# Eighteen matmuls that nobody reads, placed between a first attention layer and the routing of a soft mixture of experts

## The reference

```python
h = jnp.concatenate([tok_embed(x), txt], axis=1)               # 32 x 96 x 192
h = h + attn0(layernorm(h))                                    # 12 heads of 16
# soft mixture of experts, 64 slots
xn = rms_norm(layernorm(h), norm_weight); tok = l2_normalize(xn)
logits = einsum('sd,btd->bst', l2_normalize(slots) * scale, tok)
dispatch_w = softmax(logits, axis=-1); combine_w = softmax(logits, axis=-2)
y = einsum('btd,bst->bsd', xn, dispatch_w)
y = gelu(einsum('sio,bsi->bso', fc1_weight, y) + fc1_bias)      # 64 expert matrices 192 x 768
y = einsum('sio,bsi->bso', fc2_weight, y) + fc2_bias
h = h + einsum('bsd,bst->btd', y, combine_w)
# then a causal attention with rotary positions and a routed mixture of 8 experts
```

## Time and profile before

| | us |
|---|---|
| median of 3 runs | 1104.42 (1103.48 to 1104.73) |
| profiled execution | 1107.96 |
| its span | 1105.9 |
| TensorE busy | 854.4 |
| VectorE busy | 603.4 |
| ScalarE busy | 432.1 |
| GpSimd busy | 398.7 |
| mean granted clock of TensorE, 1 being 2.4 GHz | 0.842 |

### The profile page before, as it was taken

One profiled execution on the slowest core, in us unless ns is written; L12 is line 12 of the kernel. 1 busy time (PEld: TensorE's weight loads), 2 busy tenths in 40 slices (PEclk: granted clock), 3 DMA queues, 4 the chain that ended last, 5 costly groups with the idle time before them and its releaser, 6 DMA issues. The chain is left out here.

```text
span 1105.9 us, 23004 instructions
## 1 busy us (share of the span) xinstructions
PE 854.4 (77%) x7560; PEld 704.6 (64%) x7561; DVE 603.4 (55%) x1401; ACT 432.1 (39%) x1022; POOL 398.7 (36%) x390
## 2 busy tenths in 40 slices
PE   3599999999977980444445599889157999999994
PEld 2477887878667960222223467667156999999994
DVE  1657777777753610111111668887794656555552
ACT  5245555545554320000001047764442444444442
POOL 1345444454301300000000026674275565555552
PEclk9689999999955575666668789999557999999998
DMA  9490000000000039989994190000432333332331
GB/s 286 133 409 1 1 0 0 0 0 0 1 1 2 2 113 364 368 361 355 338 336 114 32 399 2 0 0 1 132 79 61 51 50 51 52 50 49 53 53 19
DMA packets 38126, 119.42 MB, mean 108 GB/s; under 512 B 7538, under 2 KB 28564, under 8 KB 33716
## 3 DMA queue, kind: packets, MB, share of 16 engines
q1 hardware_dynamic: 25108, 104.40, 25.6%
q0 software_dynamic: 10848, 12.67, 7.1%
q10 hardware_dynamic: 2112, 1.57, 1.0%
HBM read 105.87 MB, written 11.14 MB: 106 GB/s over the span
## 5 line engine op out<-in xcount | busy, mean ns | idle before, releaser
L1029 PE MATMUL psum<-flat,m_yT 64*32 64x384 f32 x624 | 48.0, 671 | 104.3 <-issue 103.0
L1646 POOL DMA_INDIRECT out_h<-x_ys,idx x55 | 87.3, 1587 | 98.9 <-ACT x_ys L1671 79.3
L1770 PE MATMUL psum<-w_pairs,x_h_hi 128*128 x330 | 101.7, 370 | 1.1 <-DVE x_h_lo L1698 1.1
L1029 PEld LDWEIGHTS psum<-flat,m_yT 64*32 64x32 f32 x624 | 17.7, 143 | 130.0 <-issue 130.0
L986 DVE COPY f_hid<-psum 128x384 f32<-128x384 f32 x16 | 8.9, 558 | 148.7 <-PE psum L1029 148.7
L1222 POOL MEMSET b_ones<- 96x96 f32 x1 | 0.2, 178 | 242.8 <-POOLq L122 242.8
L1772 PE MATMUL psum<-w_pairs,x_h_lo 128*128 x330 | 82.8, 251 | 0.0
L1698 DVE TENSOR_TENSOR x_h_lo<-psum,x_h_hi 128x384 fp32r<-128x384 f32 x110 | 56.3, 553 | 38.8 <-ACT x_h_hi L1667 36.8
L464 POOL TENSOR_TENSOR a_kb<-a_qk,a_hmask 96x576 f32<-96x576 f32 x64 | 72.2, 1147 | 6.2 <-ACT a_qk L497 6.2
L622 PE MATMUL psum<-a_kb,a_qk 96*96 96x384 f32 (+1 forms) x256 | 67.7, 407 | 0.0
L550 DVE TENSOR_REDUCE a_mx<-psum 96x12 f32<-96x1152 f32 x32 | 43.3, 1354 | 41.8 <-PE psum L622 41.8
(11 more groups left out here) (274 smaller groups left out, 2460.2 us busy)
## 6 DMA issues: line engine op xcount, KB each, us to landing
flat<-in_slot_w SPq DMA_DIRECT2D x27, 2304.0 KB, 21.7
ring_last<-in_slot_w SPq DMA_DIRECT2D x5, 2304.0 KB, 27.9
flat<-in_moe_w SPq DMA_DIRECT2D x1, 10752.0 KB, 29.7
flat<-in_x_patches SPq DMA_DIRECT2D x4, 1536.0 KB, 14.6
out_h<-flat SPq DMA_DIRECT2D x1, 2304.0 KB, 12.2
xtab<-flat SPq DMA_DIRECT2D x4, 576.0 KB, 4.0
m_y<-in_fc_b SPq DMA_DIRECT2D x1, 1536.0 KB, 18.4
m_y<-f_y2g ACTq DMA_DIRECT2D x16, 96.0 KB
```

Source lines behind the costliest of these rows:

```text
L1029: mm = pe.matmul(b_h[n][r][B * c:B * (c + 1), :], g.yT[rows, k, SC * gr + c, :], w1[c // 2][rows, c % 2, k, n * N2:(n + 1) * N2], start=(k ...
L1646: pool.indirect_dma_start(out=A["out"][:, :], out_offset=bass.IndirectOffsetOnAxis(ap=g.idx[:, i:i + 1], axis=0), in_=ys[:, i % 2, :], in_ ...
L1770: pe.matmul(b_y[u % 2], h_hi[:, k, :], g.w_pairs[:, :, k, bass.ds(e, 1), :].rearrange("p two a d -> p two (a d)"), start=(k == 0), stop=False)
```

## The change

A function `keep_clock` is added. It issues matmuls of the 128x128 identity with 384 columns of the ring's first buffer, into PSUM bank 3, and nobody reads what they write. It is called twice, both times on PE: with 14 at the end of `attention0`'s block, behind a wait until DVE has read the last scores, and with 4 at the start of the PE stream of `dispatch`. Nothing else changes.

```diff
+N_CLOCK = 384
...
             steps(pe, B, [(project, 1), (turn_first, 3), (score, 2), (transpose_x, 0), (attend, 3), (output, 4)])
+            pe.wait_ge(s_sub, B)
+            keep_clock(pe, g, 14)
...
+def keep_clock(pe, g, n):
+    pe.wait_ge(g.s_ring[0], 16)
+    for _ in range(n):
+        pe.matmul(g.ps[:, 3, 0:N_CLOCK], g.ident[:, :], g.ring[0][:, 0:N_CLOCK], start=True, stop=True)
...
+            keep_clock(pe, g, 4)
             few_steps(NP, [(transpose_x, 0), (products, 1)])
             few_steps(NQ, [(transpose_logits, 0), (transpose_weights, 2), (gather, 3)])
```

## The result

Over 20 executions of each kernel the median went from 1106.76 us to 1110.13; the ratio is 1.003, with a 95% interval from 1.0016 to 1.0044. So the change makes the kernel slower by 3.3 us, between 1.8 and 4.9. The forecast was +7.8 us, with a range for the time that holds the result. Part of that is luck: the forecast time of 1112.2 us counted from 1104.42, the median of three runs, while the comparison's own median before is 1106.76, which is 2.3 us more. So the time came close, and the change itself did not: +3.3 against +7.8. The profiled execution took 1111.2 us with a span of 1109.1, against a span of 1105.9 before.

The account below looks back on a forecast made before the run. The prediction took PE, at half clock through the uncovered `dispatch`, as the bound. A start 8.8 us later less 1.0 given back makes +7.8 on 1104.42, so 1112.2 us, range 1103.6 to 1114.0.

Parts of the forecast that it names:

- The bound and the stage: `dispatch`: all 82 us to `slot_ffn`'s first matmul run at 1.2 GHz, uncovered, so its end shifts the rest equally.
- The rise: From the last output matmuls at 309.62, the clock rises between 313.3 and 315.4 us, taken as 314.4.
- The fourteen: Added matmuls at `attention0`'s end: two done at 1.30 us, twelve at 0.65, ending at 322.2 us, in a 4.70 us gap.
- The barrier and the four: Start of `dispatch`: barrier opens at about 322.7, four matmuls take 2.6 us, first transpose at 325.3, 8.8 us later.
- What the high clock gives back: First part of `dispatch`: each full-clock pair gives back 0.51 us; the clock falls at some 330, four pairs give 1.0.
- My own sign: In the changed kernel's profile, the granted clock reads 0.50 again by 331 us, until `slot_ffn`'s first matmuls at 406.
- falls midway: Rival: in `dispatch`'s first part the clock falls after ten pairs or so; +4 us, 1108.4, chance 0.04.
- the likeliest case: Clock falls early in `dispatch`'s first part; +7.8 us, 1112.2, own range 1109.5 to 1113.5, chance 0.66.
- ACT's 1.35 us a pair: First part of `dispatch` at full clock: ACT's copy and two squares set the pace, 1.35 us a pair against 1.86.
- My first rival: Clock holds to the end of `dispatch`'s first part, all sixteen pairs at ACT's pace; +0.6 us, 1105.0, chance 0.18.
- The second part: Later part of `dispatch`, where PE first has only a few transposes a chunk: priced at no change, 0.
- The case on the other side: Rival: the clock holds through both parts of `dispatch`; -17.4 us in all, 1087, chance 0.08.

Follow-up runs that it names:

- the best run: Against the kernel before: two unread matmuls ahead of the barrier, four behind, one or more late in `dispatch`'s second-part steps, ACT's first part written out; 1086.95 us, ratio 0.9827.
- the run with transposes: Changed kernel with each unread 384-column matmul replaced by six unread 128x128 transposes; ratio 1.006 to the kernel before.
- the run with three chunks filled: Kernel before plus four matmuls behind the barrier, ACT's first part written out, two more in each of chunks 0 to 2 of `dispatch`'s second part; ratio 0.9985.

## Where the prediction was right and where wrong

- **The bound and the stage.** Right. `dispatch` ran at half clock, lost at the attention's end or in the gap behind it, and what moved in `dispatch` moved the end: +4.17 at `slot_ffn`'s start in the profile and +3.3 in the comparison, -19.0 and -19.4 in the best run.
- **The rise.** Right. I took 3.7 to 5.8 us from the start of the last output matmuls and chose 4.8; it rose after 3.7. In the runs with fourteen matmuls or with transposes it rose after 3.0 to 3.9, so my lower bound was too high.
- **The fourteen.** Right. Forecast 10.4 us, measured 10.0. They overran PE's gap of 4.7 us as worked out.
- **The barrier and the four.** Right in the mechanism. DVE's first instruction of `dispatch` was held until the queue had drained (324.55, idle 7.44 ahead of it), the four took 2.65 us, and the first transpose came 8.1 us later. The sum said 8.8, with bounds of 8.2 and 9.3; the measured 8.1 lies just below them, mostly because the rise came 1.1 us earlier than I took.
- **What the high clock gives back.** Wrong, and this is the step that failed: "I take it that the clock falls", some five microseconds behind the first transpose, so that four pairs give back 1.0 us. It stayed up for 12.5 us and about eight pairs ran at the high clock; 3.9 us came back in the first part instead of 1.0. My own sign, 0.50 again by 331, did not come. The forecast of +7.8 stands against +4.2 in the profile and +3.3 in the comparison. The course that the profile shows is the rival "falls midway", +4, to which I gave 0.04. The range of the likeliest case was off as well: 8.2 at the start and six fast pairs give 1110.6, not 1109.5.
- **Why that step failed.** I argued from the kind of work, transposes and short matmuls. These very pairs hold the clock: with ACT written out they did so for 22.5 us, and the run with transposes shows the same for 128x128. I also took 4.9 and 4.6 us as the time that the clock lasts behind dense matmuls. The second was read where PE had nothing at all to do from 622.89 on. In the run with the four alone it fell 1.1 us behind the last output matmul (0.65 in 312 to 316), in the changed kernel 12.4 us behind the last added one. So there is no such fixed time.
- **What makes it fall.** Before most falls PE's busy time had thinned out: 2.99 of 4 us in the changed kernel, 1.77 in the run with three chunks filled. That this is the cause is argued and not shown in full, and thinness alone does not decide. The kernel before lost the clock at 306.6 with PE busy 2.74 of the 4 us ahead; the run with the four alone, which has the same instructions and the same gaps there, was busy 2.60 of 4 us at the same place and kept it until PE stood still. In eight of the fourteen profiles the clock fell ahead of the last output matmuls, in six behind them. That holding may need less than lifting, as I had put on the other side, is borne out: in the kernel before, the same pairs with PE busy 4.00 of 4.00 never lifted the clock, and with 3.62 of 4 they held it.
- **ACT's 1.35 us a pair.** Right for seven pairs, wrong for the other nine, because I read it off the first two copies, ahead of ACT's loop. In the loop a pair takes 1.72 to 1.75 us, and 2.06 once, at the start of the second turn. Before, PE's 1.86 hid this. My first rival, with the clock up and 16 pairs at 1.35, did not happen in this code; it did with the loop written out, where the logits came at +37.23 and the sum for that rival says +38.5.
- **The second part.** Right: no chunk changed, and the clock was at half.
- **The case on the other side.** That the clock holds through both parts of the change as made is wrong: even with ACT written out it fell where PE waits at the start of the second part. With other edits it holds, and the stage then gives what the case names, but the close totals, 17.4 in the sum and 19.0 in the best run, are luck. The first part gave back 6.9 us there (logits at +30.6 instead of +37.48), where the sum had it 1.0 later. From the logits to `slot_ffn` it gained 12.2 us (51.4 to 39.2), where the sum had 16.6, because chunks took 3.91 us and not 3.4.

By the rule of the Trainium skill on idle gaps ("TensorE: Matmul & The Clock Gate", section "Why this matters for your kernels"), as I read it, the clock would hold through both parts. The trace does not agree: in the changed kernel it fell at 339.7 with no gap over 0.53 us on PE in `dispatch` up to there.

What stays open: what PE must do for a rise or a hold, why the clock falls at different places in the same instructions, and in how many executions of the runs with few added matmuls it rises. Each kernel has one profile, and for the other executions only the mean clock is known.

## What to carry to other kernels

Work that nobody reads can raise and hold TensorE's clock, but here it paid only in PE's waits: ahead of a barrier or of the step that another engine waits for, each such matmul is a delay of its full length. Ask first how long the next stage will keep the clock up by itself, and where PE thins out in it; then put the filler there, behind what others wait for. And where a clock rises, look for the engine that then sets the pace, including what its own loop costs.

## What the hardware showed that I had not expected

- Float32 transposes of 128x128 hold the full clock: 8 us of nothing else at 1.00, behind a rise to which matmuls had contributed.
- ACT's hardware loop makes a pair cost 1.72 to 1.75 us instead of 1.35, with the same copy and two squares in it: idle times of about 0.27 and 0.18 us stand between them that are not there in the written-out stream.
- The last output matmuls of the attention took 2.21 us in the profile of the kernel before and 1.19 in that of its control with ACT written out, which is the same program up to there. When the clock falls differs from execution to execution, and the first transpose followed 1.0 us earlier.
